# Idle-slot matrix products on TensorE in an eight-pair transformer kernel: 55 unread products a pair, at three places

## What is computed

```python
x = x + attn0(layernorm(x))     # q, k, v, softmax over 512 keys, w_o
x = x + ffn0(layernorm(x))      # relu(h)**2 @ w_proj
x = x + attn1(layernorm(x))
x = x + trees(layernorm(x))     # silu(logits) on the path taken, @ W_out
```

## Time and profile before

| | |
|---|---|
| time, median of 3 runs | 3384.36 us (3380.99 to 3385.28) |
| the profiled execution | 3380.93 us, its span 3379.0 us |
| busy share of the span | PE 89%, DVE 66%, ACT 57%, POOL 27% |
| mean granted TensorE clock | 0.944 |
| chain that ended last, by engine | PE 64%, DVE 24%, ACT 5% |

### The profile page before, as it was taken

One profiled execution on the slowest core, in us unless ns is written; L12 is line 12 of the kernel. 1 busy time (PEld: TensorE's weight loads), 2 busy tenths in 40 slices (PEclk: granted clock), 3 DMA queues, 4 the chain that ended last, 5 costly groups with the idle time before them and its releaser, 6 DMA issues.

```text
span 3379.0 us, 50607 instructions
## 1 busy us (share of the span) xinstructions
PE 3022.3 (89%) x20068; PEld 1375.3 (41%) x20068; DVE 2222.8 (66%) x4099; ACT 1917.0 (57%) x2559; POOL 909.1 (27%) x1206
## 2 busy tenths in 40 slices
PE   0488899989999899989999899998899989999899
PEld 0124255342643336333363435524254342633336
DVE  0785866758566676767667586675856667576764
ACT  0274654737547474565746566474754738456574
POOL 0013223142321414214241232314133141421413
PEclk9589899999989899998999989999899989999899
DMA  3000000000100001000010000100001000100000
GB/s 118 21 22 20 21 26 33 22 20 22 38 30 12 25 16 51 27 2 30 24 38 28 19 22 21 38 22 20 21 29 39 12 20 22 46 25 9 30 18 20
DMA packets 92700, 91.03 MB, mean 27 GB/s; under 512 B 15757, under 2 KB 89877, under 8 KB 92453
## 3 DMA queue, kind: packets, MB, share of 16 engines
q1 hardware_dynamic: 92465, 87.79, 7.6%
HBM read 17.48 MB, written 8.39 MB: 8 GB/s over the span
## 4 chain that ended last, share of the span: by engine, by line
PE 64%; DVE 24%; ACT 5%; SPq 3%; issue 2%; POOL 1%; DMA 1%; DVEq 0%
PE ps L995 13%; PE ps L1040 11%; PE ps L1065 10%; PE ps L1262 8%; DVE nmax L753 8%; DVE nmax L756 7%; PE ps L1020 6%; PE ps L1001 4%; PE ps L1233 3%; PE ps L1051 3%; ACT probs L524 3%; SPq L263 2%; PE ps L1008 2%; SPq L284 1%; PE ps L1253 1%
## 5 line engine op out<-in xcount | busy, mean ns | idle before, releaser
L524 ACT ACTIVATE probs<-ps 128x1024 f32<-128x1024 f32 x1024 | 1041.9, 1024 | 378.7 <-PE ps L1051 375.5
L1040 PE MATMUL ps<-kst,qst 48*128 48x512 f16 x2048 | 749.1, 409 | 145.4 <-DVE nmax L756 64.7
L753 DVE TENSOR_REDUCE nmax<-ps 128x2 f32<-128x512 f32 x1024 | 650.4, 684 | 210.9 <-PE ps L1040 204.3
L756 DVE TENSOR_REDUCE nmax<-ps 128x1 f32<-128x512 f32 x1024 | 650.3, 683 | 181.2 <-PE ps L1040 178.3
L1051 PE MATMUL ps<-qst,kst 54*128 54x512 f16 x2048 | 726.4, 406 | 5.0 <-ACT probs L524 5.0
L1065 PE MATMUL ps<-probs,vn 128*32 128x512 f32 (+1 forms) x5184 | 572.8, 515 | 6.6 <-ACT oT L512 6.6
L1040 PEld LDWEIGHTS ps<-kst,qst 48*128 48x128 f16 x2048 | 166.2, 94 | 785.0 <-DVE nmax L753 325.9
L420 POOL TENSOR_TENSOR probs<-probs 127x512 f16<-127x512 f32 (+1 forms) x256 | 292.2, 1162 | 519.7 <-ACT probs L655 519.7
L655 ACT ACTIVATE probs<-probs 127x512 f16<-127x512 f32 (+1 forms) x256 | 161.3, 630 | 350.5 <-DVE probs L949 346.8
L1262 PE MATMUL ps<-wout,probs 127*128 127x256 f16 (+1 forms) x3072 | 357.2, 273 | 0.0
L995 PE MATMUL ps<-hT,win 128*127 128x512 f16 (+1 forms) x1536 | 354.3, 380 | 2.6 <-ACT probs L631 2.6
(11 more groups left out here) (115 smaller groups left out, 3195.9 us busy)
## 6 DMA issues: line engine op xcount, KB each, us to landing
qst<-parts SPq DMA_DIRECT2D x384, 64.0 KB, 2.6
kst<-parts SPq DMA_DIRECT2D x384, 64.0 KB, 2.6
x<-in_x SPq DMA_DIRECT2D x16, 512.0 KB, 3.6
probs<-x SPq DMA_DIRECT2D x16, 512.0 KB, 3.0
out<-probs SPq DMA_DIRECT2D x16, 512.0 KB, 3.1
qst<-nrow SPq DMA_DIRECT2D x256, 12.0 KB
qst<-in_winT SPq DMA_DIRECT2D x1, 2040.0 KB
oT<-in_wfcT SPq DMA_DIRECT2D x1, 1024.0 KB
```

Source lines behind the costliest of these rows:

```text
L524: nc.scalar.activation(probs[:, g % 2, 2 * hf:2 * hf + 2, s % G, :], ps[:, 2 + 2 * hf:4 + 2 * hf, :], ACT.Exp).then_inc(exp_rd, 1)
L753: nc.vector.tensor_reduce(nmax[:, u, 2 * tt + half, :, slot], bank[tt % 2].rearrange("p (a s) -> p a s", s=BLK), AX.X, ALU.max, negate=Tru ...
L756: nc.vector.tensor_reduce(nmax[:, u, 2 * tt + half, 0, slot:slot + 1], bank[tt % 2], AX.X, ALU.max, negate=True).then_inc(max_rd, 1)
L1040: mm(bank[tt % 2], qst[lo:hi, ai % 2, e // 2, tt * P:(tt + 1) * P], kst[lo:hi, ai % 2, e // 2, :], start=True, stop=True).then_inc(max_ps, 1)
```

## The change

A function `keep_going(k, free)` issues `k` products of 512 columns (weights: the 128x128 identity `idb`; moving: the first 512 columns of `wfc`), into a bank that holds nothing at that moment. They start and stop their own sum, wait for no semaphore and raise none. No engine reads the result. Per pair there are 6, 9 and 7 between the steps of the norms after phase 2, 8 ahead of phase 4 and 12 within its steps 0 and 1, 4 in step 0 of phase 0, and, in all pairs but the last, 2, 4 and 3 at the trees' end. That makes 55 a pair (46 in the last), 431 in all. Nothing is removed or reordered.

```diff
+            def keep_going(k, free):
+                for _ in range(k):
+                    mm(free, idb[:], wfc[:, HI, 0, 0:S], start=True, stop=True)
+
...
                     if s >= G:
                         weighted(n, ai, s // G - 1, s % G, (0,) if split else (0, 1))
+                    if s == 0 or (s == 1 and nxt == 5):
+                        keep_going(4, bank[6])
                     pair_of_tiles(b, ph, n, ahead, s, 1)
+                    if s == 0 and nxt == 5:
+                        keep_going(4, bank[6])
                     if split:
...
                 attn_T(n1, 1, 1)
+                keep_going(6, bank[2])
                 pe.wait_ge(aT_hi, n1 * KD + KD)
                 pe.wait_ge(aT_lo, n1 * KD + KD)
                 projected(n1, 1, 0)
                 projected(n1, 1, 1)
+                keep_going(9, bank[2])
                 transposed(b, 4, 0)
                 transposed(b, 4, 1)
+                keep_going(7, bank[2])
                 hT_read(b, 4, 0)
...
                 project(b, 15)
+                keep_going(8, bank[2])
                 attention_even(b, 4)
...
                 tree_sum(b, TREES - 1)
                 if more:
+                    keep_going(2, bank[6])
                     lead_tiles(n4, 0, 12)
+                    keep_going(4, bank[6])
                     lead_tiles(n4, 0, 13)
+                    keep_going(3, bank[6])
```

## The result

| | before | changed |
|---|---|---|
| median | 3384.22 us (3380.99 to 3385.28) | 3350.63 us (3348.2 to 3361.14) |
| profiled execution's span | 3379.0 us | 3348.3 us |
| mean granted clock | 0.944 | 0.974 |

The ratio is 0.9908, 95% interval 0.9886 to 0.993: faster by 0.9%, inside the range, with about six tenths of the forecast gain. It lies outside the forecast's own span, 3317 to 3345, and on the 3350 of one of the rivals.

A forecast was written before the change was run, and what follows sets the result against it. TensorE ran part of the time at half rate, mean clock 0.944, mattering where VectorE waits for it. Gains of 15.2 + 17.6 + 21.7 = 54.5 us gave 3330 us, range 3309 to 3354.

The forecast's parts named there:

- the forecast's own span: Whole kernel: the time from the low and high ends of the three places' gains, 39 to 67 us.
- one of the rivals: Only norms and part of phase 4 gain, phase 0 nothing: 3358, or 3350 with phase 4's fall late; chance 0.17.
- Norms: After phase 2: 22 products keep the clock up, transposes and two units run faster; 1.9 us a pair, 15.2 in all.
- Phase 4: Its start: 20 products hold the clock through steps 0 and 1, VectorE waits less from step 2; 2.2 us a pair.
- lower end of 1.4 us: Phase 4: gain a pair if the clock falls just ahead of step 3's unit, which then costs 1.27 us again.
- Phase 0: Trees' end and phase 0: 13 products, one shorter fall stays over one or both units; 3.1 us, seven pairs, 21.7.
- its upper end: Phase 0 with all at full rate: 5.1 us a pair, VectorE waiting 0.7 us at each of two units.
- Pairs: Distance from one pair to the next: 402.7 us before, to fall to about 395.5.
- Products are in the way: Rival: exposed products delay tiles VectorE waits for; slower, 3392 with two thirds exposed, 3423 at worst; chance 0.06.
- the clock doesn't follow: Rival: the clock falls at the same places despite the products, nothing is gained; 3387 to 3392, chance 0.05.
- The argument from the eight transposes: Against the skill's claim that transposes don't engage full clock: eight transposes, 1.97 of 3.40 us, and the clock rose right after.
- using it as a bound: Whole kernel: by the skill's under 1%, at most 34 us could be had, the time no less than 3350.

The follow-up runs named there:

- e4: The change plus two products ahead of each pair of score tiles in steps 2 and 3 of phase 4 (64 in all): 3336.48 us.
- e5: e4 plus two products ahead of each pair of score tiles in steps 1 and 2 of phase 0: 3330.23 us.
- e12: e9 with two products again ahead of score tiles in phase 0's steps 1 and 2, except step 1's first pair, which keeps one: 3322.16 us.
- e9: e5 with fewer products at the trees' end, in phase 0 and in the sparse steps of phases 0 and 4: 3325.67 us.
- e3: The change with only its products at the trees' end and in step 0 of phase 0 kept: 3366.34 us.
- e1: The change with only its 22 products a pair at the norms kept: 3358.3 us.
- e11: e5 without the 22 products a pair at the norms: 3347.21 us.
- e10: The change with every count of products doubled, 862 in all: 3403.73 us.
- e8: e5 plus four products ahead of the first wait of the odd phases (64 in all): 3331.74 us.

## Why the prediction was right, and where it was not

The direction and the mechanism held: the clock follows the added products, and the gain is what other engines waited for TensorE. That the time lies in the range is owed to the range being wide. That it lies on the rival's 3350 is chance: that rival has phase 0 gain nothing, and it gained 2.7 us a pair, while phase 4 gave less than the rival and the forecast both have.

- **Norms: right.** 1.7 us a pair measured in pairs 2 to 8 (1.0 in the first), 1.9 forecast; clock, transposes and units came as described.
- **Phase 4: the term that was mis-sized.** The step "I take 2.2, nearer to the upper end, because the place in which a fall would do harm is short" gave 17.6 us and measured 4.9. The mechanism stood in the text, a fall ahead of the unit of step 3. It came in every pair, and in most stayed for 6.8 us, over the unit, the tiles behind it and the first weighted sums, not over a unit alone; so even the lower end of 1.4 us was too high in six pairs. e4 shows it, with the fall gone and 2.2 to 2.3 us gained. Steps 0 and 1 were right: no VectorE gap, the products under cover.
- **Phase 0: 2.7 us a pair for 3.1.** One fall stayed, as forecast from the earlier trace rows. But its upper end was wrong: with no fall it is 3.2 in e5, which has eight products a pair more here, and 4.1 in e12, which has one more than the change and sets them otherwise, not 5.1; the change's own 13 without a fall were not run. A fall costs about 1.5 us (e9), near the 1.27 us of one unit at half rate; VectorE's waits at the units were taken too small by 0.9 us together, and products in its way can cost 0.9 us (e5 against e12) where I had 0.2.
- **First pair and phase 1: missed.** The first pair's phase 0 had 4 products and lost 2.1 us: the clock was up 6 us earlier than before, fell in the thin step, and both units ran at half rate. These four do not bring it about by themselves: e3 and e4 have them too, their clock came up as late as before, and they lost 0.4 and 0.3 us. Phase 1 lost 1.4 us in two pairs.
- **Pairs: missed.** The distance from one phase 0 fall to the next was 399.4 or 395.9 us, 398.2 in the mean, where I had 395.5.
- **Terms taken as a sum.** The deepest fault is that each place's gain was priced by itself. e1 to e3 show that as long as any place is near a fall, changing one moves the outcome at the others. In e11's trace, where but for one short fall no other place falls, the other places do stay as they were; what the norms lose comes to 13.7 us, but unevenly by pair, so that it meets 8 times 1.7 is in part luck.
- **Rivals.** "Products are in the way" decides only when doubled (e10); "the clock doesn't follow" did not happen. The argument from the eight transposes is weaker than it was put: in the second pair the same eight stand at 982.80, and the clock stayed at 0.50 until 999.1. The Trainium skill, "TensorE: Matmul & The Clock Gate", Part 1, holds the ramp penalty to be under 1% of a typical span. It says so of the first products of a kernel; here the clock falls again in every pair, so I stretched it in using it as a bound. The change alone would stay within it with 0.9%, but e12 takes back 1.7%.

What stays open: why the clock fell at the start of phase 1 in just these two pairs, after waits of 1.05 and 1.13 us, where e12 waits up to 1.36 us at such a start without a fall; how often it falls from run to run (the change's runs spread from 3348, at a mean clock of 0.975, to 3361, at 0.969, wider than before's); in e4, e9 and e11 one fall each, at the lead tiles behind the norms of the fifth pair, where no run adds products; and one in e9 at the start of phase 5 of the third pair, behind a wait of 1.31 us. The products that e8 has there were only tried on a version that did not fall.

## What to carry to other kernels

Before pricing filler work by its gap, look past the gap: the next steps in which TensorE only feeds a slower engine decide whether the clock is still up when dense work comes. Cover all such steps or expect the fall to move to the next one, and judge one place only when the others don't fall. Give each gap no more than it holds: what fits costs little, and of the work put in past that more than half was paid here (53 of 93 us in e10), without keeping the clock up in the thin steps.

## What the runs showed of the hardware

In the changed kernel the granted clock fell after stretches in which TensorE never stood idle longer than 1.13 us at a time (start of phase 1, 1.05 and 1.13 us; phase 0, 0.81; phase 4, 0.72), so it takes no long gap for a fall: steady thin work came before them. Nor does a single wait decide it: e12 had one of 1.36 us at the start of phase 5 without a fall, and at the unfilled norms TensorE stood idle for 2.07 us in two pairs of e3 and one of e11 without one. With 22 products added at one place, which took 1.7 us a pair out of the time there, the clock was back up 10.2 us after its fall at phase 0, about 270 us later, in each of seven pairs; before it took 17.1 us, in five of the seven with 3.4 us at full rate within.
